# An attention kernel on one core: the causal mask goes from a TensorE matmul into VectorE's row maximum, and a batch element's last row stages run in the first steps of the next

## The chip, the cores and the metric

The kernel runs on one core of one Trainium2 chip. The metric is the device time of one execution in microseconds (us), taken as the median of several runs. The engines are TensorE (PE in the profile; its weight loads are PEld), VectorE (DVE), ScalarE (ACT), GpSimd (POOL) and SyncE (SP), which issues the DMAs. Each has its own queue of instructions, and they wait for each other with semaphores. SBUF is the memory on the core, and the eight PSUM banks (`bank0` to `bank7`) are where TensorE writes.

## The reference

Two layers work on x of 8 batch elements x 512 positions x 128 channels. Each is a modulated layer norm with attention and then one with a feed-forward part, both added to x. Layer 0 (an RWKV scan and a feed-forward in 6-bit numbers) isn't touched. In layer 1, attention has 16 heads and three branches that share the queries:

```python
a1 = _attn(q, k1, v1, causal=True)      # keys from a latent
a2 = _attn(q, ks, vs, causal=False)     # 32 selected keys
a3 = _attn(q, kw, vw, causal=True)      # keys made straight from x
out = g[:, 0] * a1 + g[:, 1] * a2 + g[:, 2] * a3

def _attn(q, k, v, causal):
    s = jnp.einsum('bhqd,bhkd->bhqk', q, k) * scale
    if causal:
        s = jnp.where(mask, s, jnp.finfo(s.dtype).min)
    return jnp.einsum('bhqk,bhkd->bhqd', jax.nn.softmax(s, axis=-1), v)
```

After it comes a recurrent cell over the batch elements, c = f * c + i * g, and an output tanh.

## The kernel before

Layer 1's attention is cut into units. A unit is one head, one of the two causal branches and one tile of 128 query rows; tile t sees (t+1) x 128 keys, so its scores are 128 to 512 columns wide. Four heads make a group; a group has 32 units (`GU`) in two rows of 16 (`RU`), one row per branch; a batch element has four groups, so 128 units, and there are 1024 in all. In a row the tiles come as 3, 2 for each of the four heads, and then 1, 0.

`attend(turn)` exists once for each engine and writes that engine's list by hand, step s after step s. There is no scheduler. It is called for three kinds of turn: `FIRST` (one group), `FULL` (128 units, the body of a hardware loop that runs 7 times) and `LAST` (three groups). The boundary of a turn lies one group ahead of that of a batch element. Step s holds:

- TensorE: the scores of unit s into one of three banks (L1639; a small extra matmul at L1637 for the selected keys); then the mask matmul (L1641), which adds `maskB` to the last 128 columns by multiplying it with an identity, both bf16; the products with the values for rows 11 and 19 steps back (`PV_TALL`, `PV_LOW`, L1601); the spreading of the rows' inverses (`SPREAD`, L1612); the transposes of the probabilities of unit s-2 (`T_LAG`, L1660) into bank 3 or 4; and, from a table in `group_tasks`, one fill task in bank 7 (projections for the next group, the cell and so on: L1507 to L1575; `vl` is L1553).
- VectorE: reads of bank 7 for some tasks; the row maximum of unit s (L1331), which waits for the mask's semaphore `s_qk`; the move of unit s-3's transposed probabilities out of PSUM (`D_LAG`, L1338, tiles 3, 1 and 0); the inverses of a row's sums (`INVERT`), its normalisation (`NORM`, L1314) and the addition (`ADD`, L1320).
- ScalarE: reads of bank 7; the move of tile 2 (L875); where a bank holds selected scores, their copy (L891); the exp of unit s from the bank to `Pb` in SBUF, with the row's sum by an accumulator (L895), which waits for the row maximum; the move of the spread inverses (`MOVE`, L901).

The next transposes wait until the bank that they write has been moved, so TensorE's L1660 at unit k waits for VectorE's L1338 (or ScalarE's L875) of unit k-2. In VectorE's list that move stands behind the row maximum of unit k+1. The scores of unit s wait until the exp of unit s-3 has read their bank.

Stages that lag run past a turn's last unit. Before the change each engine therefore adds steps to each turn, TensorE up to 5, ScalarE 6, VectorE 9, and only then takes the loop's jump (L1691 on TensorE, L1414 on VectorE); L1416 is VectorE's first copy in a turn.

## Time and profile before

| | |
|---|---|
| time, median of 3 runs | 2289.77 us (2286.21 to 2292.29) |
| the profiled execution's own time | 2280.42 us |
| its span | 2278.6 us |
| mean granted clock of TensorE | 0.913 of full speed |
| TensorE, VectorE, ScalarE, GpSimd busy | 85%, 59%, 49%, 28% of the span |
| layer 1's attention | about 380 to 2230 us |

The page's busy times are shares of the span. A matmul's end is modelled, and matmuls overlap, so a line's cost on TensorE is read from the starts in the timeline. "PEld L1660 <- DVE L1338" is idle time of the weight loads at line 1660 that ended when VectorE's L1338 did. "issue" is idle time for which the profile shows no cause outside the engine.

### The profile page before, as it was taken

The numbers are of one execution on the slowest core, as the hardware profiler recorded it, in microseconds if no ns is written. First come the engines' busy times: TensorE is split into PE (matmuls) and PEld (weight loads), VectorE is DVE, ScalarE is ACT, GpSimd is POOL, SyncE is SP. The second block draws the span as 40 slices with busy tenths as digits, with TensorE's granted clock in tenths as the row PEclk, the third lists the DMA queues.
The fourth block names the chain that finished last, engine by engine and source line by source line (L and its number), as shares of the span: only waits on it lengthen the run. The fifth ranks groups of instructions, "written<-read, shape, count | busy, mean of one in ns | idle before, by whom it ended". The sixth has DMA issues, their size and how long they took to land.

```text
span 2278.6 us, 41302 instructions
## 1 busy us (share of the span) xinstructions
PE 1931.2 (85%) x11644; PEld 1110.1 (49%) x11644; DVE 1349.9 (59%) x3206; ACT 1126.1 (49%) x3476; POOL 645.8 (28%) x659
## 2 busy tenths in 40 slices
PE   3333356999989998999899998999899989999995
PEld 2222123555545554555455554555555555555552
DVE  5999942556555555565655564555465645565563
ACT  1112212555546564556555655655465545555551
POOL 0232233333312331333223232323233322332200
PEclk7655665999999999999999999999999999999998
DMA  3000001111101111111111111111111111111101
GB/s 135 0 0 0 0 9 38 51 37 41 48 21 40 39 41 37 34 39 41 44 33 34 46 43 35 34 46 43 35 34 46 43 26 42 36 53 26 41 1 37
DMA packets 71354, 81.39 MB, mean 36 GB/s; under 512 B 29521, under 2 KB 37842, under 8 KB 70994
## 3 DMA queue, kind: packets, MB, share of 16 engines
q1 hardware_dynamic: 71122, 78.55, 13.4%
q8 instruction: 115, 1.88, 0.4%
q14 instruction: 117, 0.96, 0.1%
HBM read 7.70 MB, written 2.10 MB: 4 GB/s over the span
## 4 chain that ended last, share of the span: by engine, by line
PE 74%; DVE 15%; issue 7%; ACT 2%; POOL 1%; SPq 1%; DVEq 1%; DMA 0%; ACTq 0%; POOLq 0%
PE bank L1639 23%; PE bank L1660 14%; PE bank L1601 9%; PE bank L1511 4%; PE bank L1512 4%; DVE arena L1338 3%; PE bank L1641 2%; PE bank L1612 2%; PE bank L1553 2%; PE bank L1507 1%; PE bank L1549 1%; PE bank L1566 1%; DVE arena L1098 1%; DVE arena L1331 1%; PE bank L1574 1%
## 5 line engine op out<-in xcount | busy, mean ns | idle before, releaser
L1331 DVE TENSOR_REDUCE arena<-bank 128x1 f32<-128x512 f32 (+3 forms) x1024 | 501.8, 490 | 681.4 <-PE bank L1641 669.8
L1639 PE MATMUL bank<-arena 96*128 96x512 f32 (+6 forms) x2048 | 782.5, 464 | 44.3 <-issue 33.1
L895 ACT ACTIVATE arena<-bank,arena 128x512 f32<-128x512 f32 (+3 forms) x1024 | 539.7, 527 | 418.3 <-DVE arena L1331 410.9
L1660 PE MATMUL bank<-W,arena 128*128 128x128 f32 x2560 | 480.4, 286 | 38.2 <-DVE arena L1338 33.2
L1660 PEld LDWEIGHTS bank<-W,arena 128*128 128x128 f32 x2560 | 281.3, 142 | 320.9 <-issue 171.3
L1639 PEld LDWEIGHTS bank<-arena 96*128 96x128 f32 x2048 | 336.4, 196 | 189.4 <-issue 146.5
L1338 DVE COPY arena<-bank 128x512 f32<-128x512 f32 (+2 forms) x768 | 351.0, 459 | 0.0
L674 POOL TENSOR_TENSOR arena<-arena,one 128x512 f32<-128x512 f32 x64 | 66.8, 1043 | 846.3 <-DVE arena L1305 836.6
L1641 PE MATMUL bank<-maskB,identB 128*128 128x128 bf16 x1024 | 229.0, 224 | 0.0
L1601 PE MATMUL bank<-arena 128*32 128x256 f32 (+1 forms) x3072 | 222.7, 362 | 3.3 <-DVE arena L1338 2.0
L895 ACT ACTIVATION_READ_ACCUMULATOR arena<-bank,arena 128x1 f32 x1024 | 204.5, 200 | 0.0
L875 ACT ACTIVATE arena<-bank 128x384 f32<-128x384 f32 x256 | 126.0, 492 | 122.4 <-PE bank L1660 122.3
L625 POOL TENSOR_TENSOR arena<-arena,W 128x512 f32<-128x512 f32 x64 | 69.9, 1092 | 342.3 <-ACT arena L817 342.3
L1641 PEld LDWEIGHTS bank<-maskB,identB 128*128 128x128 bf16 x1024 | 100.8, 98 | 115.4 <-issue 87.4
L891 ACT ACTIVATE arena<-bank 128x32 f32<-128x32 f32 (+1 forms) x384 | 78.5, 204 | 142.0 <-DVE arena L1331 140.5
L1462 PE MATMUL bank<-W,arena 128*128 128x128 f32 x160 | 34.0, 349 | 123.3 <-ACT arena L775 53.5
L1601 PEld LDWEIGHTS bank<-arena 128*32 128x32 f32 x3072 | 61.0, 109 | 115.3 <-issue 96.8
L1511 PE MATMUL bank<-arena,LW 96*128 96x512 f32 x192 | 109.3, 652 | 3.1 <-ACT arena L817 2.5
L1512 PE MATMUL bank<-arena,W 128*128 128x512 f32 x192 | 103.8, 623 | 4.3 <-ACT arena L817 3.6
L634 POOL TENSOR_TENSOR arena<-arena 128x512 f32<-128x512 f32 x64 | 81.3, 1271 | 44.0 <-DMA arena<-arena 36.5
L817 ACT ACTIVATE arena<-bank 128x512 f32<-128x512 f32 x128 | 76.6, 599 | 27.1 <-PE bank L1512 9.9
L1462 PEld LDWEIGHTS bank<-W,arena 128*128 128x128 f32 x160 | 23.3, 178 | 135.9 <-ACT arena L775 55.1
(263 smaller groups left out, 2304.2 us busy)
## 6 DMA issues: line engine op xcount, KB each, us to landing
arena<-arena SPq DMA_DIRECT2D x896, 64.0 KB, 2.0
arena<-arena SPq DMA_DIRECT2D x64, 128.0 KB, 2.4
W<-wide SPq DMA_DIRECT2D x1, 3538.0 KB, 12.9
X<-x SPq DMA_DIRECT2D x8, 256.0 KB, 5.4
out<-arena SPq DMA_DIRECT2D x8, 256.0 KB, 2.2
arena<-arena SPq DMA_DIRECT2D x96, 16.0 KB, 1.9
LW<-lat SPq DMA_DIRECT2D x1, 768.5 KB, 13.9
arena<-mods SPq DMA_DIRECT2D x1, 768.0 KB, 4.4
```

Of the source, the lines that this page charges most:

```text
L634: step(pool.tensor_tensor(stX1, rt[:, 2], rt[:, 3], ALU.subtract))
L875: A(turned(turn, k), turned_bank(turn, k), ACT.Copy).then_inc(s_pa, 1)
L891: made = A(p2h[:, h, tiles], scores, ACT.Copy)
L895: A(Pb[:, s % 4, 0:n], bank[s % 3][:, lo:lo + n], ACT.Exp, bias=nmax[:, s:s + 1], accum_out=lsum[:, c:c + 1]).then_inc(s_p, 1)
L1331: v.tensor_reduce(nmax[:, s:s + 1], bank[s % 3][:, lo:lo + n], AX_X, ALU.max, negate=True).then_inc(s_max, 1)
L1338: CP(turned(turn, k), turned_bank(turn, k)).then_inc(s_pd, 1)
L1511: return MM(dst[:], LW[0:QL, col:col + P], latT[0:QL], start=True, stop=True)
L1512: return MM(dst[:], w("wink", col, P), hTc, start=True, stop=True)
L1601: last = MM(bank[5][rows, low * 2 * P:low * 2 * P + n], V[a][turn.g(q) % 2][:, c, rows], PT[low][:, h, c * 2 * P:c * 2 * P + n], start=(c ...
L1639: MM(bank[s % 3][:, 0:lo + n], query(t), Kb[a][0:QD, g % 2, h, skip:skip + lo + n], start=True, stop=False)
L1641: MM(bank[s % 3][:, lo + t * P:lo + n], identB[:], maskB[:], start=False, stop=True).then_inc(s_qk, 1)
L1660: last = pe.transpose(bank[3 + k % 2][:, c * P:(c + 1) * P], Pb[:, k % 4, c * P:(c + 1) * P], ident)
```

## The change

The mask matmul goes, with its two bf16 tiles and the two copies that made them in set-up. In their place the mask lies in SBUF as 512 columns (zero but for the last 128), loaded with the wide input. VectorE's row maximum becomes one `tensor_tensor_reduce`: it adds mask and scores, multiplies by -1, writes the result to `Pb` and takes the minimum, which is the negated row maximum. It is built as two instructions, the fused one and the read of its accumulator, which carries the semaphore. Ahead of it stands an increment of a semaphore of its own (`s_seen`), which takes the waits: for the scores, and for the transposes of unit s-4, since `Pb` is now written here. ScalarE's exp reads and writes `Pb` in place, with scale -1. The scores of unit s now wait for the row maximum of unit s-3, and only where ScalarE copies selected scores from the bank for the exp.

The second part: a turn has no added steps, but for the last one. Stages that lag run in the first steps of the next turn, with negative row and unit numbers. The banks of the scores are renumbered for it, and one fill task (`vl` of group 0) is put three steps earlier.

```diff
@@ -33,7 +33,7 @@
         ("wfT", P), ("ufT", P), ("wiT", P), ("uiT", P), ("wcT", P), ("ucT", P), ("wo2T", P), ("uoT", P),
-        ("cos", T), ("sin", T), ("mask", P), ("iota", KEEP)]
+        ("cos", T), ("sin", T), ("mask", T), ("iota", KEEP)]
 WIDE_AT, _at = {}, 0
@@ -74,7 +74,7 @@
     if g == 0:
-        steps, proj = {"op": 11, "p2T": 23, "o2": 25}, (1, 2, 4, 7, 8, 13, 15, 27, 33)
+        steps, proj = {"op": 11, "p2T": 23, "o2": 25}, (1, 2, 4, 7, 8, 13, 15, 27, 30)
         extra = [] if first else [(17, "z4T"), (20, "gf"), (21, "gi"), (24, "gc")]
@@ -126,6 +126,9 @@
         self.first, self.last = tasks is FIRST, tasks is LAST
+        self.n0 = 0 if self.first else -GU
+        self.n1 = len(self.units) + (ADD - RU + 1 if self.last else 0)
+        self.c0 = (NG - 1) * GU if self.first else 0
 
@@ -148,7 +151,16 @@
         q, h, a, t = self.units[s]
-        return s - s % RU + (NT - 1 - t) * HG + h
+        return self.c0 + s - s % RU + (NT - 1 - t) * HG + h
+
+    def score_bank(self, s):
+
+        return (s if self.first else s + GU) % 3
+
+    def rows(self, s, at):
+
+        r, late = divmod(s - at, RU)
+        return r, late, self.n0 // RU <= r < len(self.units) // RU
 
@@ -227,8 +239,6 @@
         impd = sb("impd", [P, B, B])
-        identB = sb("identB", [P, P], BF16)
-        maskB = sb("maskB", [P, P], BF16)
         ones_row = sb("ones_row", [1, P])
@@ -864,12 +875,12 @@
                 p2h = p2.rearrange("p (t j k) -> p j t k", t=NT, j=HG)
-                for s in range(n_units + MOVE - RU + 1):
+                for s in range(turn.n1):
                     task = turn.at(s - 1, "act")
...
                     k = s - T_LAG
-                    if 0 <= k < n_units and MOVER[turn.units[k][3]] == "act":
+                    if turn.n0 <= k < n_units and MOVER[turn.units[k][3]] == "act":
                         act.wait_ge(s_pT, u0 + (k + 1))
@@ -877,9 +888,6 @@
                         act.wait_ge(s_max, u0 + (s + 1))
-                        if not (turn.first and s < 4):
-
-                            act.wait_ge(s_pT, u0 + (s - 3))
                         if lo:
@@ -887,15 +895,15 @@
                             m = 2 if t == 0 else 1
-                            scores = bank[s % 3][:, 0:m * (KEEP + P)].rearrange("p (m x) -> p m x", m=m)[:, :, 0:KEEP]
+                            scores = bank[turn.score_bank(s)][:, 0:m * (KEEP + P)].rearrange("p (m x) -> p m x", m=m)[:, :, 0:KEEP]
                             made = A(p2h[:, h, tiles], scores, ACT.Copy)
...
                         c = turn.col(s)
-                        A(Pb[:, s % 4, 0:n], bank[s % 3][:, lo:lo + n], ACT.Exp, bias=nmax[:, s:s + 1],
+                        A(Pb[:, s % 4, 0:n], Pb[:, s % 4, 0:n], ACT.Exp, bias=nmax[:, s:s + 1], scale=-1.0,
                           accum_out=lsum[:, c:c + 1]).then_inc(s_p, 1)
-                    r, late = divmod(s - MOVE, RU)
-                    if 0 <= r < n_units // RU and late == 0:
+                    r, late, known = turn.rows(s, MOVE)
+                    if known and late == 0:
                         act.wait_ge(s_sp, turn.r0 + (r + 1))
@@ -1168,8 +1176,6 @@
             step(TS(w("krsw", HALF, HALF), w("krsw", HALF, HALF), 1.0 / HEADS, None, ALU.mult))
-            step(CP(identB[:], w("ident")))
-            step(CP(maskB[:], w("mask")))
             step.settle()
@@ -1300,7 +1306,7 @@
                         v.wait_ge(s_ix, r0 + (r - 1))
-                    step(v.reciprocal(inv[:, r % 2], lsum[:, r * RU:(r + 1) * RU]))
+                    step(v.reciprocal(inv[:, r % 2], lsum[:, turn.c0 + r * RU:turn.c0 + (r + 1) * RU] if r >= 0 else lsum[:, NG * GU - RU:]))
                     step.settle()
@@ -1328,17 +1334,22 @@
                         v.wait_ge(s_qk, u0 + (s + 1))
-                        v.tensor_reduce(nmax[:, s:s + 1], bank[s % 3][:, lo:lo + n], AX_X, ALU.max, negate=True).then_inc(s_max, 1)
+                        if not (turn.first and s < 4):
+
+                            v.wait_ge(s_pT, u0 + (s - 3))
+                        v.sem_inc(s_seen, 1)
+                        v.tensor_tensor_reduce(Pb[:, s % 4, 0:n], bank[turn.score_bank(s)][:, lo:lo + n], w("mask", T - n), -1.0, 3e38,
+                                               ALU.add, ALU.min, nmax[:, s:s + 1]).then_inc(s_max, 1)
                     k = s - D_LAG
-                    if 0 <= k < n_units and MOVER[turn.units[k][3]] == "dve":
+                    if turn.n0 <= k < n_units and MOVER[turn.units[k][3]] == "dve":
                         v.wait_ge(s_pT, u0 + (k + 1))
...
                     for at, row_part in ((INVERT, row_inverted), (NORM, row_normed), (ADD, row_added)):
-                        r, late = divmod(s - at, RU)
-                        if 0 <= r < n_units // RU and late == 0:
+                        r, late, known = turn.rows(s, at)
+                        if known and late == 0:
                             row_part(r)
@@ -1626,28 +1637,29 @@
                                 pe.wait_ge(s_krB, turn.b * (16 * HG) + 16 * HG)
-                        if s >= 3:
-
-                            pe.wait_ge(s_p, u0 + (s - 2))
+                        if s >= 3 or not turn.first:
+
+                            before = s - 2 if s < 2 else s - 3
+                            _, _, a3, t3 = turn.units[before]
+                            pe.wait_ge(s_p if scores_at(a3, t3) else s_max, u0 + (before + 1))
                         lo = scores_at(a, t)
...
 
-                            MM(bank[s % 3][:, lo + n:lo + n + KEEP], query(NT - 1), Kb[0][0:QD, g % 2, h, 0:KEEP],
+                            MM(bank[turn.score_bank(s)][:, lo + n:lo + n + KEEP], query(NT - 1), Kb[0][0:QD, g % 2, h, 0:KEEP],
                                start=True, stop=True)
-                        MM(bank[s % 3][:, 0:lo + n], query(t), Kb[a][0:QD, g % 2, h, skip:skip + lo + n],
-                           start=True, stop=False)
-                        MM(bank[s % 3][:, lo + t * P:lo + n], identB[:], maskB[:], start=False, stop=True).then_inc(s_qk, 1)
+                        MM(bank[turn.score_bank(s)][:, 0:lo + n], query(t), Kb[a][0:QD, g % 2, h, skip:skip + lo + n],
+                           start=True, stop=True).then_inc(s_qk, 1)
                     for low, at, parts in ((0, PV_TALL, 4), (1, PV_LOW, 2)):
-                        r, c = divmod(s - at, RU)
-                        if 0 <= r < n_units // RU and c < parts:
+                        r, c, known = turn.rows(s, at)
+                        if known and c < parts:
                             values(r, low, c)
-                    r, late = divmod(s - SPREAD, RU)
-                    if 0 <= r < n_units // RU and late == 0:
+                    r, late, known = turn.rows(s, SPREAD)
+                    if known and late == 0:
                         spread(r)
                     k = s - T_LAG
-                    if 0 <= k < n_units:
+                    if turn.n0 <= k < n_units:
                         t = turn.units[k][3]
@@ -1720,7 +1732,7 @@
     sin = np.tile(np.sin(angle).T, (HG, 1)).astype(np.float32)
-    mask = np.where(np.arange(P)[None, :] > np.arange(P)[:, None], MASKED, 0.0).astype(np.float32)
+    mask = np.where(np.arange(T)[None, :] - (T - P) > np.arange(P)[:, None], MASKED, 0.0).astype(np.float32)
     cols = [d["L0_c"].T, d["L1_c"].T]
```

VectorE in the loop, four steps from a turn's start. Before:

```order
L1337 ISA [waits probsT_in_psum]
L1338 COPY arena<-bank3 128x4x128 [waits half_pv_done]
L1330 REGISTER_ALU
L1331 TENSOR_REDUCE arena<-bank1 128x1 [waits scores_ready]
L1330 REGISTER_ALU
L1331 TENSOR_REDUCE arena<-bank2 128x1 [waits scores_ready]
L1338 COPY arena<-bank3 128x4x128 [waits half_pv_done,probsT_in_psum]
```

After:

```order
L1336 REGISTER_ALU
L1341 ISA arena<-bank0,W 128x512 [waits scores_ready,probsT_in_psum]
L1341 ISA arena 128x1
L1336 REGISTER_ALU
L1341 ISA arena<-bank1,W 128x384 [waits scores_ready,probsT_in_psum]
L1341 ISA arena 128x1
L1349 COPY arena<-bank3 128x4x128 [waits half_pv_done,probsT_in_psum]
L1336 REGISTER_ALU
L1341 ISA arena<-bank2,W 128x512 [waits scores_ready,probsT_in_psum]
```

Behind every row maximum there is now a second, one-column instruction, and the move of unit s-3 comes behind both. The increment that holds the wait is not a row of its own here.

TensorE at the end of the loop's body (bank 4 and 3: transposes, 7: fill, 5: values, 6: spread). Before, in the steps past the last unit:

```order
L1658 REGISTER_ALU [waits probs_ready]
L1660 MATMUL bank4<-W,arena 128x128 [waits probsT_moved_by_dve]
...
L1553 MATMUL bank7<-LW,arena 128x128 [waits shared_bank_read_by_act]
...
L1601 MATMUL bank5<-arena 32x256 [waits probsT_moved_by_act,probsT_moved_by_dve]
...
L1612 MATMUL bank6<-W,arena 128x128 [waits row_inverses_moved,row_inverses_repeated]
...
L1601 MATMUL bank5<-arena 32x128 x4
L1691 REGISTER_ALU
L1691 COMPARE_AND_BRANCH
```

After, where the jump comes directly behind unit 125's transposes:

```order
L1564 MATMUL bank7<-LW,arena 128x128 [waits shared_bank_read_by_act]
...
L1652 MATMUL bank0<-arena 128x128 [waits row_max_ready]
L1664 REGISTER_ALU
L1670 REGISTER_ALU [waits probs_ready]
L1672 MATMUL bank4<-W,arena 128x128 [waits probsT_moved_by_dve]
L1703 REGISTER_ALU
L1703 COMPARE_AND_BRANCH
```

The last two units' transposes, the two value products and the spread have gone from the end. TensorE at the start of the loop's body, before:

```order
L1639 MATMUL bank0<-arena 128x512 [waits shared_key_moved_odd]
L1641 MATMUL bank0<-maskB,identB 128x128
...
L1511 MATMUL bank7<-arena,LW 128x512 [waits shared_bank_read_by_dve]
L1639 MATMUL bank1<-arena 128x416
L1641 MATMUL bank1<-maskB,identB 128x128
L1639 MATMUL bank2<-arena 128x512
L1641 MATMUL bank2<-maskB,identB 128x128
...
L1660 MATMUL bank3<-W,arena 128x128 [waits probsT_moved_by_dve]
...
L1511 MATMUL bank7<-arena,LW 128x512 [waits shared_bank_read_by_act]
L1639 MATMUL bank0<-arena 128x416 [waits probs_ready]
```

And after:

```order
L1652 MATMUL bank2<-arena 128x512 [waits row_max_ready]
...
L1672 MATMUL bank3<-W,arena 128x128 [waits probsT_moved_by_dve]
...
L1522 MATMUL bank7<-arena,LW 128x512 [waits shared_bank_read_by_dve]
...
L1652 MATMUL bank0<-arena 128x416 [waits row_max_ready]
...
L1672 MATMUL bank4<-W,arena 128x128 [waits probsT_moved_by_dve]
L1652 MATMUL bank1<-arena 128x512 [waits row_max_ready]
...
L1672 MATMUL bank3<-W,arena 128x128 [waits probsT_moved_by_dve]
...
L1652 MATMUL bank2<-arena 128x416 [waits row_max_ready]
...
L1612 MATMUL bank5<-arena 32x256 [waits probsT_moved_by_act]
...
L1623 MATMUL bank6<-W,arena 128x128 [waits row_inverses_moved]
...
L1672 MATMUL bank4<-W,arena 128x128 [waits probsT_moved_by_dve,probs_ready]
...
L1652 MATMUL bank0<-arena 128x512 [waits probs_ready]
```

They stand now between the scores of the new turn's first steps: transposes of units 126 and 127 in steps 0 and 1, values and spread in steps 3 and 4.

## Rows read from the trace of the kernel before

**Rows 1.** The page's sections 1 and 4: busy times, and the chain's shares.
```profile
PE 1931.2 (85%) x11644; PEld 1110.1 (49%) x11644; DVE 1349.9 (59%) x3206; ACT 1126.1 (49%) x3476; POOL 645.8 (28%) x659
...
PE 74%; DVE 15%; issue 7%; ACT 2%; POOL 1%; SPq 1%; DVEq 1%; DMA 0%; ACTq 0%; POOLq 0%
```

**Rows 2.** Windows of 200 us: each engine's busy us (x instructions), granted clock, DMA.
```profile
600.00:800.00 200.00, 188.17 (x1153) 108.44 (x1154) 113.63 (x270) 112.00 (x354) 63.79 (x61) 0.97 0.14 36
```

**Rows 3.** Waits of the whole span: idle us, times, longest; L1639 by shape.
```profile
PEld bank L1660 <- DVE arena L1338: 110.7, 189, 1.1
...
PEld bank L1601 <- DVE arena L1338: 17.5, 34, 1.1
...
L1639 PE MATMUL bank<-arena 96*128 96x512 f32 x512 | 282.4, 634 | 44.3 <-issue 33.1 <-ACT arena L862 9.5 <-ACT arena L895 1.2
```

**Rows 4.** TensorE's timeline near a turn's end: the mask and the next transpose.
```profile
893.29 0.22 PE L1641 MATMUL bank<-maskB,identB 128*128 128x128 bf16 x1
893.35 0.28 PE L1660 MATMUL bank<-W,arena 128*128 128x128 f32 x1
```

**Rows 5.** Timeline around one wait (start us, us, engine, line).
```profile
680.58 0.22 PE L1641 MATMUL bank<-maskB,identB 128*128 128x128 bf16 x1
...
680.84 0.56 DVE L1331 TENSOR_REDUCE arena<-bank 128x1 f32<-128x384 f32 x1 [1.58 <-PE bank L1641]
...
681.31 0.68 DVE L1338 COPY arena<-bank 128x512 f32<-128x512 f32 x1
...
681.83 0.22 PE L1641 MATMUL bank<-maskB,identB 128*128 128x128 bf16 x1
...
682.04 0.42 PEld L1660 LDWEIGHTS bank<-W,arena 128*128 128x128 f32 x4 [0.54 <-DVE arena L1338]
```

**Rows 6.** VectorE's groups by shape: busy us, mean ns of one, idle before.
```profile
L1331 DVE TENSOR_REDUCE arena<-bank 128x1 f32<-128x512 f32 x256 | 176.7, 690 | 208.5 <-PE bank L1641 203.6
...
L1314 DVE TENSOR_TENSOR arena<-bank,arena 128x512 f32<-128x512 f32 x64 | 43.7, 683 | 20.9 <-ACT arena L901 20.9
...
L1252 DVE SCALAR_TENSOR_TENSOR arena<-arena 128x512 f32<-128x512 f32 x8 | 5.5, 682 | 12.2 <-ACT arena L855 12.2
```

**Rows 7.** Timelines: four of VectorE's smallest; ScalarE's accumulator read and its next.
```profile
2233.11 0.37 DVE L948 BATCH_NORM_AGGREGATE small<-small 128x2 f32<-128x6 f32 x4
...
684.76 0.21 ACT L895 ACTIVATION_READ_ACCUMULATOR arena<-bank,arena 128x1 f32 x1
684.86 0.61 ACT L817 ACTIVATE arena<-bank 128x512 f32<-128x512 f32 x1
```

**Rows 8.** Timelines of TensorE and VectorE at L1221, outside the loop and inside.
```profile
2117.72 1.02 PE L1560 MATMUL bank<-W,arena 128*128 128x512 f32 x2
...
2118.78 0.69 DVE L1221 TENSOR_TENSOR arena<-arena,bank 128x512 f32<-128x512 f32 x1 [0.74 <-PE bank L1560]
...
713.52 1.02 PE L1560 MATMUL bank<-W,arena 128*128 128x512 f32 x2
...
714.70 0.69 DVE L1221 TENSOR_TENSOR arena<-arena,bank 128x512 f32<-128x512 f32 x1 [0.79 <-PE bank L1560]
```

**Rows 9.** Timeline where VectorE's move ends just ahead of its reader.
```profile
721.40 0.28 DVE L1338 COPY arena<-bank 128x128 f32<-128x128 f32 x1
...
721.87 0.28 PE L1660 MATMUL bank<-W,arena 128*128 128x128 f32 x1
```

**Rows 10.** TensorE's timeline at a turn's end, with a jump of the loop.
```profile
894.22 0.56 PE L1660 MATMUL bank<-W,arena 128*128 128x128 f32 x3 [0.60 <-DVE arena L1338]
...
903.16 1.22 PE L1639 MATMUL bank<-arena 96*128 96x512 f32 x1 [5.78 <-issue]
```

**Rows 11.** The loop's branch on TensorE's queue: ns min/median/max, first and last start.
```profile
L1691 PEldq COMPARE_BRANCH  x7: 76/3347/3692, 660.8 to 2074.1; - x7
```

**Rows 12.** TensorE's timeline: first scores after the turn's end without a jump.
```profile
2075.16 1.12 PE L1639 MATMUL bank<-arena 96*128 96x512 f32 x2
```

**Rows 13.** Window after the restart: engines' busy us, then TensorE's clock.
```profile
903.10:911.30 8.20, 8.14 (x16) 3.77 (x17) 1.94 (x3) 2.14 (x6) 0.00 (x0) 0.50 0.00 0
```

5 lines of the change are left out of this document (3 added, 2 removed).

## The prediction

> **What bounds the kernel now.** I read the first section of the page, then the chain that ended last, then the table of windows, to find the engine that sets the end; then the waits, to see who holds it up; then the timeline around one of each kind of place. The first section and the chain say TensorE: busy 85% of the span, and 74% of the chain [rows 1]. The windows say where: in the attention of layer 1 TensorE is busy 188 of 200 us, VectorE 114 and ScalarE 112 [rows 2]. Those two are only waited for at single places, so an average tells nothing of them, and the waits do. TensorE's weight loads wait for VectorE's move of the transposed probabilities (L1338) 189 times at the transposes and 34 times at the values: 223 places in 1024 units, 27 or 28 per turn of 128 units [rows 3]. The full-width scores matmul (L1639) sat idle for ScalarE's exp only 1.2 us in all [rows 3], so freeing the scores' bank earlier, which the change also does, is worth about a microsecond and I leave it out.
>
> **Part 1, the mask leaves TensorE.** A mask matmul shows 0.22 us busy, but matmuls overlap: from its start to that of the transpose behind it are 893.29 to 893.35, 0.06 us [rows 4]. Over all such pairs of the trace it is 58 to 60 ns, so 0.059. Its weight load lies beside other matmuls. 1024 x 0.059 would be 60 us. At each of the 223 places where TensorE waits for VectorE's move one mask lies in the wait's shadow, as the one at 681.83 does (TensorE sits idle from then until 682.04 whether it is there or not) [rows 5]. So 1024 - 223 = 801 masks, **-47 us**.
>
> **Part 2, VectorE's row maximum becomes longer.** Take the place at 680.58 [rows 5]. Mask starts 680.58, row maximum of that unit 680.84, the move of an earlier unit stands behind it in VectorE's queue and starts at 681.31, takes 0.68, and the transpose that needed the bank free starts at 682.04, after 0.54 idle. The mask at 680.58 is on this path, ahead of the row maximum, and is among the 801; with it gone the wait is on the scores' matmul. What is new is what stands between the scores' end and the move: the fused instruction in the place of the plain one, its accumulator read as a second instruction, and the wait, which now sits on a semaphore increment of its own ahead of it. I call the sum of the new parts p, per unit.
>
> The main instruction: an addition of a bank and an SBUF tile of 512 columns takes 683 ns, the row maximum of 512 columns 690 [rows 6]. I take them equal. That also holds for the write of the sums to SBUF, which the 683 has and the 690 has not.
>
> The accumulator read, x: no VectorE instruction in the trace reads an accumulator. Below it lie VectorE's smallest: four aggregates in 0.37, one of which takes 0.15, so 0.07 from start to start [rows 7]. Above it lies ScalarE's own accumulator read: 0.19 to 0.21 long, though ScalarE's next instruction starts 0.10 after it [rows 7]. So x is 0.07 to 0.19, and I take 0.07, because start to start is what the queue behind it pays, and both rows say 0.07 to 0.10 there.
>
> The wait, e: the profile has the same instruction with both kinds of wait. At L1221 outside the loop the wait is on the instruction, and it starts 0.04 after TensorE's matmul ends (2117.72 + 1.02 to 2118.78); inside the loop a sequencer operation takes the wait, and it starts 0.15 after (713.52 + 1.02 to 714.70), with VectorE idle for 0.79 before [rows 8]. All 28 in the loop show 0.13 to 0.16 and all 4 outside it 0.04. So e is up to 0.11; I take 0.08, since an increment needs no address worked out. The low end of e is nothing. The increment's second wait, for the transposes of unit s-4, comes two steps after TensorE issued them and is never the last; queued behind the increment are the fused instruction, on which ScalarE's exp waits, and the move, on which TensorE does.
>
> p = 0.15, between 0.07 and 0.30. 223 x 0.15 = **+33 us**. Six more places per turn wait for VectorE's or ScalarE's reads of the shared bank, which stand behind the same instruction: 48 x 0.14 = **+7 us**. Then there are near misses: at 721.40 the move takes 0.28 and ends at 721.68, and the transpose that needs it starts at 721.87 [rows 9]. The trace has about 5 such places per turn with under 0.19 us left; each lies closer by p plus the mask that TensorE no longer does: 40 x 0.1 = **+4 us**.
>
> I work this out as lengthening of waits that exist, not as load, because VectorE has room: 1024 x 0.15 is 154 us on 1350 busy [rows 1].
>
> **Part 3, the late stages of a turn's last rows run in the next turn.** Before the change TensorE does at a turn's end, after its last normal transpose at 893.35 [rows 4], the last transposes at 894.22 (0.60 idle for VectorE's move), then a fill task, values, spread and values again, and then nothing until 903.16, for 5.78 us put down to "issue" [rows 10]. That gap is the loop's jump: TensorE's queue shows a branch of 3.35 us, by the median of 7 [rows 11], and where the same stages end without a jump the next turn's first scores, at 2075.16, have no idle before them [rows 12]. After the restart the clock is at 0.50 (1.2 GHz) for 8.2 us [rows 13]. The branch is issued when the work before it is queued, so the last of it, about 1 us of spread and value matmuls, runs while the jump goes on. Moved past the jump, it costs its own time that was covered, some of it at half clock, and it gives back the 0.60 of waiting and a part of the drain: I put each of the 7 jumps at +0.2, **+1.4 us**. The two turn boundaries without a jump lose the 0.60 wait and the thin tail: -0.8 each, **-1.6 us**. Together nothing. What follows on the other engines: the row inverses (L1303), NORM (L1314) and ADD (L1320) enter VectorE's list in steps 0, 7 and 8 of the next turn behind the first row maxima, ScalarE's MOVE in step 5, and GpSimd's and SyncE's work is behind them as before; no DMA is added or moved past another on SyncE's queue. If their cover were gone, the 0.68 of a NORM 14 times would be 10 us; the first steps have it, since TensorE runs there at half clock. The mask becomes 384 columns wider in a load during set-up, and two set-up copies go: within 0.3 us.
>
> **Sum.** -47 + 33 + 7 + 4 + 0 = -3 us against the profiled execution of 2280.4 us (span 2278.6). That execution lies 9.4 us under the median of the runs, 2289.8, so the same difference on the median gives **2286**. It breaks even at p of 0.16 to 0.17, hence nearly everything hangs on p.
>
> **Rivals.**
>
> *The extra VectorE time is covered.* With p at its lower end, 0.07: 223 x 0.07 = 16, the six places +3, no new near misses: -28 us, 2262. For it: if x is 0.07 and the increment takes the wait at no cost. Against it: the 0.15 at L1221 in the loop.
>
> *Slower: the accumulator read holds VectorE.* If the read takes its whole length (0.19) as ScalarE's shows, and the wait 0.09, p is 0.28: 62 + 13 + 7 - 47 = +36 us, 2326. It is at the same 223 places, where the move stands behind the read in VectorE's queue; it decides from p of 0.20, where the sum is slower by more than 0.3%.
>
> *Half rate.* If the fused instruction took twice as long per column, it would add 0.13 to 0.53 us, 0.33 on average: 223 x 0.33 = 74 us more, and with new waits 2345 to 2400. For it stands only that it reads two tensors and accumulates. Against it: the 683 ns of a bank and an SBUF tile, and of L1252, which reads two float tensors of SBUF in 682 [rows 6]; neither accumulates. The Trainium skill ("Vector Engine (DVE) Microarchitecture Reference", section 7, "Points that are easy to get wrong") says that the scalar-tensor-tensor form with two SBUF sources that are not bf16 halves throughput, because no port is left for the accumulator. L1252's 682 ns speaks against that for the form without accumulator, and here one source is a bank; no run here shows the case with one. By the page's rule, were it to apply, the time would be this rival's 2345 or more; without it the sum is as above.
>
> *The gap at the jump goes.* If it came from the thin tail and not the jump, 5.8 us of idle and some 4 us of half clock would go 7 times: -69 us, 2220. Against it is the branch of 3.35 us itself [rows 11].
>
> **Chances.** Forecast 0.58 (p from 0.11 to 0.21: -13 to +15 us, 2277 to 2305), covered 0.15, slower by the read 0.17, half rate 0.05, gap gone 0.05. The range, 2258 to 2328, holds the forecast, the slower rival's own sum and most of the covered one; the last two rivals lie outside. A measurement of this kernel can tell 0.3% from nothing, 7 us. Faster by more: covered 0.15, gap 0.05, and of the forecast the part with p under 0.13, 0.20: 0.40. Slower by more: 0.17, 0.05, and the part with p over 0.195, 0.10: 0.32. Within: 0.28.
>
> **What would show it.** The move's start behind the row maximum's, 0.47 before for 384 columns, should be 0.47 plus x. The places where TensorE waits for the move: 223 to about 260, the wait about p longer. The chain without L1641, with a larger share of VectorE. All seven gaps at the jumps still there, 5 us or more. A gap under 1 us, a fused instruction of over 0.75 us at 512 columns, or a read that holds the queue 0.15 or more would make the prediction wrong.

## The result, and the profile after

The changed kernel is slower: 2318.07 us by the median of four runs (2311.4 to 2327.2), against 2288.9 for the kernel before. The ratio is 1.0129, with a 95% interval of 1.0084 to 1.0175. The forecast was 2286, no change, with a chance of 0.32 for slower. The time lies in the range, but it moved the other way than forecast, by more than the measurement's uncertainty. Each ratio here and below is taken over executions within 1.5% of their kernel's fastest; only in e13_one_wait does that leave any out, three of ten and the profiled one among them. The profiled execution took 2312.3 us with a span of 2310.5, so the two spans differ by 31.9 us, and the comparison of the traces below is about these.

The page of after, sections 1 and 4:

```profile
PE 1911.7 (83%) x10620; PEld 1069.9 (46%) x10620; DVE 1367.5 (59%) x4228; ACT 1163.8 (50%) x3476; POOL 645.1 (28%) x659
...
PE 69%; DVE 17%; issue 8%; ACT 3%; DVEq 1%; POOL 1%; SPq 1%; DMA 0%; ACTq 0%; POOLq 0%
```

TensorE is busy for 20 us less than in [rows 1], and its share of the chain has gone from 74% to 69% while VectorE's has risen from 15% to 17%. The same in a window of the attention (compare [rows 2], 188 us busy of 200):

```profile
600.00:800.00 200.00, 182.77 (x1043) 101.91 (x1043) 114.67 (x374) 115.85 (x354) 63.73 (x61) 0.96 0.14 36
```

The waits for VectorE's move, which is now at L1349, against the 189 and 34 of [rows 3]:

```profile
PEld bank L1672 <- DVE arena L1349: 226.0, 286, 2.7
...
PEld bank L1612 <- DVE arena L1349: 31.1, 34, 1.4
```

They are 320 places, not 223, and of the larger group the mean wait is 0.79 us where it was 0.59. VectorE's groups by shape, against [rows 6]:

```profile
L1341 DVE CUSTOM_DVE_ANT_0 arena<-bank,W 128x512 f32<-128x512 f32 x256 | 176.7, 690 | 209.6 <-PE bank L1652 151.1 <-PE bank L1672 56.9
...
L1341 DVE DVE_READ_ACCUMULATOR2_ANT arena<- 128x1 f32 x1024 | 85.1, 83 | 0.0
```

The fused instruction of 512 columns takes 690 ns, just as long as the plain row maximum did: half rate is out. Its accumulator read lasts 83 ns. One wait in the timeline, to be read beside [rows 5]:

```profile
920.37 0.52 PE L1652 MATMUL bank<-arena 96*128 96x160 f32 x2
...
921.11 0.29 DVE L1341 CUSTOM_DVE_ANT_0 arena<-bank,W 128x128 f32<-128x128 f32 x1 [1.06 <-PE bank L1652]
...
921.33 0.08 DVE L1341 DVE_READ_ACCUMULATOR2_ANT arena<- 128x1 f32 x1
921.33 0.69 DVE L1349 COPY arena<-bank 128x512 f32<-128x512 f32 x1
...
922.07 0.44 PE L1672 MATMUL bank<-W,arena 128*128 128x128 f32 x2 [0.36 <-DVE arena L1349]
```

The scores end at 920.89 (920.37 + 0.52), and the fused instruction starts at 921.11, 0.22 later. In [rows 5] the mask ended at 680.80 and the row maximum started at 680.84. The accumulator read and the move both start at 921.33: the read stands beside the move and hardly ahead of it. TensorE gets going at 922.07.

Over all units where VectorE had been idle for more than 0.3 us, the median from the scores' end to the start of the row maximum is 37 ns before and 225 ns after. From its start to the move's start it is 208 and 216 ns at 128 columns, 607 and 617 at 512. So the new time per unit is **0.19 of waiting and 0.01 of accumulator read**.

Where in a turn it went can be read from the starts of the 1024 row maxima in both traces. Turns start with one copy on VectorE (columns: count, ns min/median/max, first and last start); before and after:

```profile
L1416 DVE COPY gtc<-gates x7: 169/169/169, 437.7 to 1845.1; 128x3 f32 x7
```

```profile
L1427 DVE COPY gtc<-gates x7: 158/169/171, 430.1 to 1865.2; 128x3 f32 x7
```

That is 234.6 us per turn before and 239.2 after. Of the 4.6 us more, the last eight units and the first eight of the next turn give back 4.2; the units around the fourth part of the third group (units 56 to 63) take 5.2; all the others take 3.5 together. TensorE's granted clock explains the middle figure. The timeline of VectorE, GpSimd and TensorE there, before and then after:

```profile
1003.85 1.51 DVE L1214 TENSOR_SCALAR arena<-W,rankT 128x32 f32<-128x32 f32 x4
...
1004.19 1.12 POOL L643 TENSOR_TENSOR arena<-arena,W 64x512 f32<-64x512 f32 x1 [4.70 <-ACT arena L812]
...
1005.28 1.08 POOL L644 TENSOR_TENSOR arena<-arena,W 64x512 f32<-64x512 f32 x1
...
1005.43 0.69 DVE L1221 TENSOR_TENSOR arena<-arena,bank 128x512 f32<-128x512 f32 x1
...
1006.24 0.29 DVE L1331 TENSOR_REDUCE arena<-bank 128x1 f32<-128x128 f32 x1
1006.45 0.68 DVE L1338 COPY arena<-bank 128x512 f32<-128x512 f32 x1
...
1007.19 0.44 PE L1660 MATMUL bank<-W,arena 128*128 128x128 f32 x2 [0.79 <-DVE arena L1338]
```

```profile
1003.06 2.42 DVE L1220 TENSOR_SCALAR arena<-W,rankT 128x32 f32<-128x32 f32 x4
...
1003.28 1.12 POOL L654 TENSOR_TENSOR arena<-arena,W 64x512 f32<-64x512 f32 x1 [4.79 <-ACT arena L823]
...
1004.36 1.08 POOL L655 TENSOR_TENSOR arena<-arena,W 64x512 f32<-64x512 f32 x1
...
1005.40 0.68 DVE L1227 TENSOR_TENSOR arena<-arena,bank 128x512 f32<-128x512 f32 x1
...
1006.38 0.29 DVE L1341 CUSTOM_DVE_ANT_0 arena<-bank,W 128x128 f32<-128x128 f32 x1 [0.30 <-DVE arena L1227]
...
1006.89 0.69 DVE L1349 COPY arena<-bank 128x512 f32<-128x512 f32 x1 [0.21 <-issue]
...
1007.63 0.67 PE L1672 MATMUL bank<-W,arena 128*128 128x128 f32 x2 [2.27 <-DVE arena L1349]
```

The four selections of L1214 (L1220 after) take 1.51 us before and 2.42 after. GpSimd's two operations (POOL) begin 0.34 us behind the selections' start before and 0.22 behind it after, so one selection or two fall beside them, and each of these lasts 1.1 us. The shared bank's read and the row maximum follow, the move comes last, and TensorE waits 2.27 us for it. Then the granted clock (the third number from the end of a window's row), first before, then after:

```profile
1007.20:1013.70 6.50, 6.50 (x61) 5.23 (x62) 2.19 (x8) 1.97 (x7) 0.60 (x1) 1.00 0.00 0
1013.70:1017.10 3.40, 3.40 (x24) 1.30 (x23) 2.68 (x11) 0.49 (x3) 0.00 (x0) 0.50 0.05 10
```

```profile
1005.42:1007.62 2.20, 0.00 (x0) 0.00 (x0) 1.69 (x6) 0.53 (x3) 1.28 (x2) 1.00 0.01 4
1007.70:1024.70 17.00, 17.00 (x88) 12.43 (x89) 5.02 (x23) 3.61 (x12) 0.00 (x0) 0.50 0.03 5
```

Before, the clock is at 0.50 (1.2 GHz) for 3.4 us here. After, it falls right behind the idle 2.2 us and stays down for 17 us, in which TensorE runs 88 matmuls, 32 of them of 32 columns. Added up over the attention, the stretches at 0.50 are 85 us before and 147 after. The seven turns of after show what a long stretch costs: units 8 to 120 take 201 us in the one turn that has none in its third group, 205 in the one with 6.8 us of it, and 207 to 209 in the five with 13.7 or 17.1. That fits half of the stretch's length, as it must be if TensorE's work takes twice as long there. So the 62 us more are worth some 31 us (an estimate): about as much as the whole difference of the spans, the other terms cancelling each other.

At the jumps the opposite happened:

```profile
897.36 0.28 PE L1672 MATMUL bank<-W,arena 128*128 128x128 f32 x1
900.38 1.22 PE L1652 MATMUL bank<-arena 96*128 96x512 f32 x1 [2.74 <-issue]
```

The gap of 5.78 us in [rows 10] is 2.74 here; the six gaps sum to 33.1 us before and 18.2 after.

### The profile page after: what moved, and what is told of

Read it like the earlier page. It is cut to its first block, busy times and chain, and to the rows that moved or that the text cites. A ratio compares the mean times of both kernels' runs of the same rounds, so it can differ in the third digit from the quotient of the medians.

```text
span 2310.5 us, 40290 instructions
## 1 busy us (share of the span) xinstructions
PE 1911.7 (83%) x10620; PEld 1069.9 (46%) x10620; DVE 1367.5 (59%) x4228; ACT 1163.8 (50%) x3476; POOL 645.1 (28%) x659
## 4 chain that ended last, share of the span: by engine, by line
PE 69%; DVE 17%; issue 8%; ACT 3%; DVEq 1%; POOL 1%; SPq 1%; DMA 0%; ACTq 0%; POOLq 0%
PE bank L1652 21%; PE bank L1672 14%; PE bank L1612 9%; DVE arena L1349 4%; PE bank L1522 4%; PE bank L1523 4%; DVE arena L1341 3%; PE bank L1623 2%; PE bank L1564 2%; PE bank L1545 2%; PE bank L1518 1%; PE bank L1577 1%; PE bank L1560 1%; DVE arena L1106 1%; PE bank L1585 1%
## 5 line engine op out<-in xcount | busy, mean ns | idle before, releaser
L1341 DVE CUSTOM_DVE_ANT_0 arena<-bank,W 128x512 f32<-128x512 f32 (+3 forms) x1024 | 502.0, 490 | 711.4 <-PE bank L1652 573.4
L903 ACT ACTIVATE arena<-arena 128x512 f32<-128x512 f32 (+3 forms) x1024 | 572.8, 559 | 442.5 <-DVE arena L1341 439.2
L1672 PE MATMUL bank<-W,arena 128*128 128x128 f32 x2560 | 487.1, 288 | 97.1 <-DVE arena L1349 92.0
L1672 PEld LDWEIGHTS bank<-W,arena 128*128 128x128 f32 x2560 | 306.2, 142 | 464.3 <-DVE arena L1349 226.0
L1652 PEld LDWEIGHTS bank<-arena 96*128 96x128 f32 x2048 | 341.1, 199 | 174.6 <-issue 149.7
L1349 DVE COPY arena<-bank 128x512 f32<-128x512 f32 (+2 forms) x768 | 356.2, 464 | 2.0 <-issue 1.5
L1612 PE MATMUL bank<-arena 128*32 128x256 f32 (+1 forms) x3072 | 227.6, 369 | 8.3 <-DVE arena L1349 7.7
L903 ACT ACTIVATION_READ_ACCUMULATOR arena<-arena 128x1 f32 x1024 | 194.8, 190 | 0.0
L1473 PE MATMUL bank<-W,arena 128*128 128x128 f32 x160 | 37.5, 379 | 122.2 <-ACT arena L786 52.7
L645 POOL TENSOR_TENSOR arena<-arena 128x512 f32<-128x512 f32 x64 | 81.4, 1271 | 39.0 <-DMA arena<-arena 31.9
L1473 PEld LDWEIGHTS bank<-W,arena 128*128 128x128 f32 x160 | 26.3, 195 | 135.3 <-ACT arena L786 54.3
L1341 DVE DVE_READ_ACCUMULATOR2_ANT arena<- 128x1 f32 x1024 | 85.1, 83 | 0.0
L649 POOL TENSOR_TENSOR arena<-arena 128x512 f32<-128x512 f32 x64 | 81.3, 1270 | 5.0
## 6 DMA issues: line engine op xcount, KB each, us to landing
W<-wide SPq DMA_DIRECT2D x1, 3730.0 KB, 13.3
```

Of the source, the lines that this page charges most:

```text
L645: step(pool.tensor_tensor(stX1, rt[:, 2], rt[:, 3], ALU.subtract))
L649: pool.tensor_tensor(stX2, rt[:, 0], rt[:, 1], ALU.add).then_inc(s_rope, 1)
L903: A(Pb[:, s % 4, 0:n], Pb[:, s % 4, 0:n], ACT.Exp, bias=nmax[:, s:s + 1], scale=-1.0, accum_out=lsum[:, c:c + 1]).then_inc(s_p, 1)
L1341: v.tensor_tensor_reduce(Pb[:, s % 4, 0:n], bank[turn.score_bank(s)][:, lo:lo + n], w("mask", T - n), -1.0, 3e38, ALU.add, ALU.min, nmax[: ...
L1349: CP(turned(turn, k), turned_bank(turn, k)).then_inc(s_pd, 1)
L1612: last = MM(bank[5][rows, low * 2 * P:low * 2 * P + n], V[a][turn.g(q) % 2][:, c, rows], PT[low][:, h, c * 2 * P:c * 2 * P + n], start=(c ...
```

## The experiments

**The two parts apart.** `e1_stages` has the moved stages alone, `e2_mask` the mask on VectorE alone.

```diff
 e1_stages, against after (its other lines put back the mask's two tiles and the exp from the bank)
...
-v.sem_inc(s_seen, 1)
-v.tensor_tensor_reduce(Pb[:, s % 4, 0:n], bank[...][:, lo:lo + n], w("mask", T - n), ...)
+v.tensor_reduce(nmax[:, s:s + 1], bank[turn.score_bank(s)][:, lo:lo + n], AX_X, ALU.max, negate=True)
...
+MM(bank[turn.score_bank(s)][:, lo + t * P:lo + n], identB[:], maskB[:], start=False, stop=True)
```

> Only the second part of the change: the late row stages run in the next turn's first steps, the mask stays a TensorE matmul. The prediction put this part at nothing (within 3 us of before). The trace of after says otherwise: around a jump a turn is 4.2 us shorter, 2.65 of them idle (the gap of 5.8 became 2.7) and the rest half clock. If that is the stages' doing, this kernel is 25 to 32 us faster than before, near 2260. If the long half-clock stretch at the third group of a turn (17 us from 1007.7 in after, 3.4 us in before) comes from the stages, it is here too and the time is near 2285.

`e2_mask` is the kernel before with the VectorE, ScalarE and set-up hunks of the change and TensorE's new wait ahead of the scores, and without its hunks on `n0`, `n1`, `rows` and `score_bank`:

```diff
 e2_mask, against before
-v.tensor_reduce(nmax[:, s:s + 1], bank[s % 3][:, lo:lo + n], AX_X, ALU.max, negate=True)
+v.sem_inc(s_seen, 1)
+v.tensor_tensor_reduce(Pb[:, s % 4, 0:n], bank[s % 3][:, lo:lo + n], w("mask", T - n), ...)
...
-MM(bank[s % 3][:, lo + t * P:lo + n], identB[:], maskB[:], start=False, stop=True)
```

> Only the first part: mask added by VectorE with the row maximum, turns with their extra steps as before. Theory of the wait (VectorE starts 0.22 us behind the scores' end instead of 0.04, at about 320 places): 22 to 27 us slower without any change of the clock, near 2313. Theory of the clock (the same part also makes TensorE sit idle 2.3 us in the third group, and the half-clock stretch behind it grows from 3.4 to 17 us): 28 us more, near 2340. If the clock's fall came from the moved stages, this kernel keeps before's 3.4 us and stays near 2313.

Measured: e1_stages 2267.2 us, ratio to before 0.9888 (0.9853 to 0.9923); e2_mask 2324.8, ratio 1.0145 (1.0104 to 1.0185). So the first part loses 1.4% and the second gains 1.1%, where the prediction had -3 us and nothing. In e1_stages all units between 8 and 112 of a turn take the same time as before, to 0.01 us in eight units, but for the third group's clock (4.9 us at 0.50 for 3.4, by the mean of seven turns); the gain is at the turns' ends alone. In e2_mask the long stretch of half clock is there (13.7 us in most turns, 160 us in all), and with half the length of its half-clock stretches taken off each, the units 8 to 120 of a turn take 2.1 us more than before. The clock's fall therefore comes from the mask's part.

**The price of the mask and of the increment.**

```diff
 e4_nomask, against before
-           start=True, stop=False)
-MM(bank[s % 3][:, lo + t * P:lo + n], identB[:], maskB[:], start=False, stop=True).then_inc(s_qk, 1)
+           start=True, stop=True).then_inc(s_qk, 1)
 e5_inc, against before
+v.sem_inc(s_seen, 1)
 v.tensor_reduce(nmax[:, s:s + 1], bank[s % 3][:, lo:lo + n], AX_X, ALU.max, negate=True).then_inc(s_max, 1)
```

> Before without the mask matmul, and so without the causal mask in the result: the price of the masks on TensorE alone. The prediction's term is 801 masks at 0.059 us, 47 us, so 2243. If masks also shorten the path scores to row maximum to move at the waits, up to 60 us, 2230. If TensorE's waits for VectorE swallow them, under 25 us.

> Before with one instruction more in VectorE's list: a semaphore increment of its own ahead of each row maximum, which takes the wait for the scores. All else as before, the mask on TensorE. The prediction's e was 0.08 us per unit: 223 places, 18 us and a few for new waits, near 2312. The trace of after shows the fused instruction 0.22 us behind the scores' end, 0.18 more than before: 40 us and 10 to 20 for new waits, near 2345, and more if the clock falls longer. If the 0.18 belongs to the fused instruction and not to the increment, under 10 us.

Measured: e4_nomask 2230.0 us, ratio 0.9723 (0.9687 to 0.9760), 63 us by the ratio and 58 by the medians; e5_inc 2356.3, ratio 1.0285 (1.0244 to 1.0327), 65 us slower. So 1024 semaphore increments on VectorE's queue cost as much as the 1024 mask matmuls on TensorE. Its place in the timeline of e5_inc:

```profile
1026.99 0.22 PE L1643 MATMUL bank<-maskB,identB 128*128 128x128 bf16 x1
...
1027.36 0.42 DVE L1333 TENSOR_REDUCE arena<-bank 128x1 f32<-128x256 f32 x1 [0.48 <-PE bank L1643]
```

The mask ends at 1027.21 and the row maximum starts at 1027.36; the median over the idle places is 0.155 us, 0.12 more than before. With the half clock taken off as above, the units 8 to 120 of a turn take 3.7 us more, 30 us in eight turns (222 places wait for the move, and 222 x 0.12 is 27); the half clock, 174 us against 85, makes up the rest. Both masks and increment thus have a price on the path near what their steps in the timeline show, and then a second one through the clock that only the increment has (88 us at half clock in e4_nomask).

**The second wait on the increment.** In after it also waits for unit s-4's transposes; `e13_one_wait` leaves that wait out.

```diff
 e13_one_wait, against after
-if not (turn.first and s < 4):
-    v.wait_ge(s_pT, u0 + (s - 3))
 v.sem_inc(s_seen, 1)
```

> After with the increment waiting for the scores alone; its second wait, for the transposes of unit s-4, is left out, since TensorE has ended those before the scores that it waits for. In after the fused instruction starts 0.225 us behind the scores' end (median), with one wait on the increment and a plain row maximum 0.155. If the second wait makes the difference, 0.155 here, and with about 320 waits for VectorE some 20 us less than after, near 2295. If the fused instruction makes it, 0.225 and the time of after, 2318.

Measured: 2288.8 us by the median of ten runs that lie far apart (2263.6 to 2302.1), ratio to before 0.9983 (0.9954 to 1.0013). The median from scores to fused instruction is 0.196 us. So of the 0.19 us that after adds there, 0.12 belongs to the increment, 0.03 to its second wait and 0.04 to the fused instruction. (At 112 of after's 656 idle places the profile names the transposes of L1672 as the last to be waited for; by the median the fused instruction starts 0.225 us behind the scores' end there too.) These 0.03 us move the ratio from 1.0129 to 0.9983. Neither expectation fits: the start is between the two, and the gain is more than 0.03 us at 304 waits. The clock can make up the difference from turn to turn. TensorE's idle in the third group is 1.92 us here, and in the trace two turns of seven pass it without the long half clock and take 231 and 232 us, where the other five take 236 to 241. That trace is of an execution of 2300.4 us; how many turns fell in the shorter ones isn't known.

**What lets the clock fall.**

```diff
 e8_pick, against after
-if g == 2 and at == 24:
-    for j in range(NT):
-        last = pick(turn.nb, j)
...
+if g == 2 and 20 <= at < 20 + NT:
+    last = pick(turn.nb, at - 20)
...
```

> After with VectorE's four selections of the third group (L1220) one per step in steps 20 to 23, not all four in step 24, where two of them took 1.1 us each beside GpSimd's work and the shared bank's read and the row maximum stood behind them. Theory of the clock: TensorE's idle 2.3 us there is what lets the clock fall for 13.7 to 17.1 us; without it the stretch is 3.4 us or none, and the kernel is 25 to 30 us faster than after, near 2290. Rival: the fall comes from the work itself (32 matmuls of 32 columns) at whatever idle: the stretch stays and the gain is the 0.9 us per turn of the stalled selections, under 10 us.

Measured: 2288.8 us (2282.4 to 2307.2), ratio to before 1.0024 (0.9996 to 1.0051), 29 us faster than after. The place in its timeline, and the clock behind it:

```profile
1002.92 0.69 DVE L1227 TENSOR_TENSOR arena<-arena,bank 128x512 f32<-128x512 f32 x1 [1.37 <-PE bank L1571]
...
1003.91 0.29 DVE L1341 CUSTOM_DVE_ANT_0 arena<-bank,W 128x128 f32<-128x128 f32 x1 [0.30 <-PE bank L1652]
...
1004.41 0.69 DVE L1349 COPY arena<-bank 128x512 f32<-128x512 f32 x1 [0.21 <-issue]
...
1005.16 0.44 PE L1672 MATMUL bank<-W,arena 128*128 128x128 f32 x2 [1.40 <-DVE arena L1349]
```

```profile
1005.20:1020.00 14.80, 13.90 (x102) 8.80 (x103) 8.69 (x37) 6.42 (x20) 1.07 (x2) 1.00 0.06 10
```

TensorE still idles 1.40 us, but in this turn the clock stays at 1.00 through the same 32-column matmuls. Over the traces, one execution of each kernel, stretches of 13.7 or 17.1 us at 0.50 follow this point in none of the seven turns with 0.79 us of idle (before, e1_stages, e9_pad), 0.91 (e4_nomask) or 1.40 (e8_pick), in three with 1.49 (e6_move_first, below), in five with 1.75 (e5_inc), five with 1.92 (e13_one_wait), six with 1.97 (e2_mask) and five with 2.27 (after). So the long fall came only behind the longer idle here, and not behind every one; with the shorter idle the same work shows 3.4 us, none, or 6.8 (three turns of e1_stages). Two of e8_pick's ten executions took 2307 us at a mean clock of 0.904, against 2282.9 and 0.911 for the traced one; what the clock did in them isn't known. The Trainium skill ("SBUF — State Buffer", "Who interferes with whom") says that a tensor_scalar in a 2-port mode and a GpSimd instruction lock each other out for a whole instruction. After's trace agrees as far as it goes: the selection that starts at 1003.36 ends at 1004.44, just behind GpSimd's operation (1003.28 to 1004.40), and takes 1.08 us instead of 0.23. That the selections run in such a mode isn't shown.

**The gap at the jump.** In before one more load of instructions falls between the jump and the first scores (q8 is a queue that loads instructions; columns: packets, MB, share; the window is 900.2 to 903.1):

```profile
q8 instruction: 1, 0.02, 2.7%
```

`e9_pad` adds 24 increments that nobody waits for, ahead of the loop on TensorE, and nothing else.

```diff
+for _ in range(24):
+    pe.sem_inc(s_pad, 1)
 with pe.Fori(0, B - 1) as i:
     attend(Turn(FULL, i))
```

> Before with 24 semaphore increments, that nobody waits for, in TensorE's list just ahead of the loop: nothing else. In before a load of instructions (16 KB, 900.48 to 901.73 in the trace) stands between the loop's jump and the first scores, and TensorE starts at 903.16, 3.06 us after the last wait of its sequencer; in the kernels whose TensorE list has another length it starts 0.1 us after. Theory of the code's position: the loop's top lies near the end of a loaded piece of code, and 24 more instructions ahead of it shift it into the next, so the gap goes from 5.2-5.9 to about 2.8 and the kernel is 15 to 30 us faster, near 2265. Theory of the stages (the gap shrinks because the late stages are gone from the end): the gap stays above 5 and the time within 5 us of before.

Measured: 2272.7 us, ratio 0.9926 (0.9900 to 0.9951): 24 instructions more make the kernel 17 us faster. Its timeline at the same jump:

```profile
897.42 0.43 PE L1602 MATMUL bank<-arena 128*32 128x128 f32 x8
900.58 0.69 PE L1640 MATMUL bank<-arena 96*128 96x512 f32 x1 [2.73 <-issue]
```

All gaps of e9_pad are 2.7 to 3.2 us, with every stage where it was, and the half clock behind the jump lasts 6.8 us instead of 10.2. The loads' times agree with the theory. At each of before's six jumps the branch ends 3.0 to 3.5 us ahead of the first scores, and a load on q8 runs between, ending 1.2 to 1.4 us ahead of them. In e9_pad the branch ends 0.6 us ahead, and that load starts only behind the first scores' start. The increments aren't free: at the loop's entry, where before has no such gap, e9_pad has one of 3.1 us and 6.8 us of half clock. The kernels with before's TensorE list (e5_inc, 5.5 to 6.0, and e11_move_first_only below, 5.2 to 6.2) keep the long gap; those whose list has another length (e4_nomask and e2_mask, 2.9 to 4.4) have a shorter one without moved stages. The six gaps sum to 17.2 us in e9_pad and 17.0 in e1_stages. So most of what the second part gained is the position of the loop's top in the loaded code. The Trainium skill ("Advanced Engine Details and Errata", "ISA Cache") gives 16 KB, 256 instructions, as the size of a line of the instruction cache. The load in the trace agrees: it is one packet of 16 KB, 0.02 MB when rounded. Between e1_stages and e9_pad 0.4% is left for the stages themselves, at intervals that overlap.

**The order on VectorE.** If the increment and the row maximum only hurt because the move stands behind them, the move can go first.

```diff
 e6_move_first, against after: the block of the move stands ahead of the row maximum, and goes from behind it
+k = s - D_LAG
+if turn.n0 <= k < n_units and MOVER[turn.units[k][3]] == "dve":
+    ...
+    CP(turned(turn, k), turned_bank(turn, k)).then_inc(s_pd, 1)
 if s < n_units:
     ...
     v.sem_inc(s_seen, 1)
```

`e7_stages_move_first` has the same swap against e1_stages, `e11_move_first_only` against before; there the block stands ahead of the plain row maximum.

> After with VectorE's move of unit s-3 ahead of the fused row maximum of unit s, not behind it. Theory of the wait: the increment and the row maximum cost TensorE time only because the move stands behind them, so the 320 waits go, and with them the 2.3 us idle in the third group and the long half-clock stretch: 60 us or more faster than after, near 2240. Rival: the waits only change sides, since the row maximum now stands behind the move and the exp comes late for its transposes: within 15 us of after.

> The stages moved, the mask on TensorE, and VectorE's move ahead of the row maximum: the same swap of two instructions where there is no increment. Theory of the wait: 209 places with 0.6 us of wait on the weight loads go in part, 20 to 50 us faster than the stages alone (2267). Rival as in the run before: within 10 us of 2267.

> Before with VectorE's move ahead of the row maximum and nothing else. The same swap was worth 88 us on the stages-moved kernel with the mask on TensorE (2267 to 2179) and 135 us on after. If it is worth the same here, 2200. If the moved stages are needed for it, clearly above 2215.

| kernel | move behind the row maximum | move first |
|---|---|---|
| before | 2289 | 2222.6, ratio 0.9699 (0.9676 to 0.9722) |
| e1_stages | 2267 | 2178.7 (e7), ratio 0.9522 (0.9506 to 0.9537) |
| after | 2318 | 2183.0 (e6), ratio 0.9539 (0.9493 to 0.9585) |

The waits for the move, in e6_move_first and then e7_stages_move_first:

```profile
PEld bank L1672 <- DVE arena L1339: 60.6, 102, 1.9
...
PEld bank L1612 <- DVE arena L1339: 23.2, 35, 1.2
```

```profile
PEld bank L1675 <- DVE arena L1346: 56.9, 128, 0.8
...
PEld bank L1614 <- DVE arena L1346: 6.1, 8, 0.9
```

In e6_move_first these are 137 places and 84 us of weight loads' idle, where after had 320 and 257; in e7_stages_move_first 136 and 63, where e1_stages had 209 and 118. On after and on e1_stages the gain, 135 and 88 us, is more than the expectations had: the increment's 0.19 us no longer stands ahead of the move, and most of the old waits of 0.6 us go with it.

On before it is less: 67 us, not the 88 of e1_stages, and 2222.6 lies above the 2215 from which the expectation called the moved stages needed. The traces put the difference at the jumps. The units 8 to 120 of a turn take 190 us in both e11_move_first_only and e7_stages_move_first, but the six gaps sum to 34.3 us in the first and 12.8 in the second. With the move first, then, the second part of the change is worth 44 us, not 21. How much of that is again the code's position wasn't tested.

**All together.** `e10_move_first_pick` is e6_move_first with the edit of e8_pick; `e12_stages_move_pick` is e7_stages_move_first with that edit, so the mask is on TensorE.

> After with VectorE's move ahead of the row maximum and the four selections one per step. The move alone gave 2183, with half-clock stretches of 13.7 us left in the third group of some turns. If these hang on VectorE's crowded step as in after, they go: 20 us faster, near 2163, and faster than the same order with the mask on TensorE (2179). If they hang on the work itself, 2175 to 2185.

> The stages moved, VectorE's move first, the selections one per step, and the mask still a TensorE matmul: the same as the fastest kernel so far (2167) but for where the mask is added. If the mask matmul costs its 60 us (58 measured by leaving it out of before) wherever VectorE isn't waited for, this is 2167 plus 30 to 60, near 2210. The kernel with the mask on TensorE and the old selections took 2179, with half-clock stretches of 3.4 us only, so the selections can give little: theory of the remaining waits, 2170 to 2180, so that the mask's move is worth 5 to 15 us even then.

Measured: e10_move_first_pick 2166.8 us, ratio 0.9453 (0.9423 to 0.9483); e12_stages_move_pick 2177.8, ratio 0.9525 (0.9507 to 0.9544). The first is the fastest kernel of this study, 5.5% faster than before. As the first of its expectations had it, none of its third groups has a stretch of 13.7 us (three of seven in e6_move_first). The page of e10 and a stretch of its timeline:

```profile
PE 1834.3 (85%) x10620; PEld 1059.8 (49%) x10620; DVE 1370.0 (63%) x4228; ACT 1146.6 (53%) x3476; POOL 645.2 (30%) x659
...
PE 71%; DVE 12%; issue 9%; ACT 5%; POOL 1%; DVEq 0%; SPq 0%; DMA 0%; ACTq 0%; POOLq 0%
```

```profile
916.29 0.64 PE L1612 MATMUL bank<-arena 128*32 128x256 f32 x8
916.59 0.42 DVE L1348 CUSTOM_DVE_ANT_0 arena<-bank,W 128x256 f32<-128x256 f32 x1 [0.33 <-PE bank L1652]
...
916.86 0.44 PE L1672 MATMUL bank<-W,arena 128*128 128x128 f32 x2
...
917.33 0.42 DVE L1339 COPY arena<-bank 128x256 f32<-128x256 f32 x1 [0.32 <-PE bank L1672]
```

The move at 917.33 now follows the transposes at once, and the fused instruction runs beside TensorE's work. Adding the mask on VectorE is worth 0.7% here by the ratios (0.5%, 11 us, by the medians). With the old order it cost 1.4% on before and 2.4% with the stages moved (1.0129 against 0.9888), and with the move first but the old selections it gives nothing (2183.0 against 2178.7). It doesn't reach the 50 to 60 us that leaving out the masks gave on before. The units 8 to 120 of a turn take 187.8 us in e10 and 190.0 in e12, but the gaps at the jumps (21.4 us against 13.3) and the half clock over the attention (65 us at 0.50 against 44) take back a part.

## Why the prediction was wrong

- **The masks, -47 us.** Right within its size. e4_nomask gave 58 to 63 us, of which 11 are the gaps at the jumps (33 us before, 22 there), so about 50. The price of 0.059 us was read from masks with a transpose behind them; the trace has 366 with a value product behind them, where start to start is 0.15, and the prediction didn't look at those.
- **x, 0.07 us for the accumulator read.** It was 0.01 from start to start. The bound from VectorE's smallest instructions was too high, and the upper end, from ScalarE's read, was far off. The page "VectorE: DVE Perf Modes" of the Trainium skill has the read as an instruction of its own ("Two Vector instructions with no wait between them"): it is, with 83 ns, and costs the queue nearly nothing.
- **e, 0.08 us for the wait.** It was 0.19. The row at L1221 showed 0.11 [rows 8], and I went below it with a reason of my own; the increment alone has 0.12. That two waits on one increment and the fused instruction add 0.07 was shown nowhere in the trace of before.
- **p, 0.15.** It was 0.20, just at the point that the slower rival named as deciding. That rival had the right place (the move behind the row maximum, at the 223 waits) and nearly the right time, 2326, but the wrong carrier: the read holds nothing, the wait does.
- **The near misses, 40 places.** There were 97 more waits. The prediction counted places with under 0.19 us left, and let each come closer by p and one mask. The runs separate the two: with the increment alone there are 222 places (e5_inc), without the masks 254 (e4_nomask), with the whole first part 331 (e2_mask). So the new waits come above all where TensorE is faster. That the masks of several units add up ahead of a wait would explain it, but no run shows that.
- **The clock.** It was in the sum only behind the jumps. This is the step that failed by most: a change of the clock elsewhere stood in the sum as nothing, and 62 us more at 0.50 made it about 31 us. The window in [rows 13] showed what half clock does, and the 3.4 us at 1013.7 in each turn of before showed that the third group sits near the fall; the prediction looked at neither as something that the change could move. That longer waits are paid twice, once as idle and once as clock, was missing.
- **Part 3, nothing.** The boundaries gave 1.1%. The step that failed here was to take all 5.78 us as the jump because the branch took 3.35 [rows 10, 11]: the branch ends at 899.6 and TensorE starts at 903.16, and the 3.5 us between had no cause in my account. The rival "the gap goes" was given 0.05 on that ground, and half of it came true, though for the code's position and not for the thin tail. Also, there are six jumps back, not seven: the shortest branch, 76 ns [rows 11], is the loop's exit.
- **The total.** The sum was -47 for the masks, +44 for the waits, 0 for the jumps and 0 for the clock. The traces have some -50, -15 for idle at the jumps and +31 for the clock; the spans' +32 then leaves 66 for the waits (an estimate, the remainder). The masks were right, p was 25% low, and the last two terms were absent. They are opposite in sign and each many times the forecast difference, so that the result lies only 1.4% from the forecast is luck.

## What to carry to other kernels

Ask of every instruction that is made longer what stands behind it in its own queue, and whether that could stand ahead: here the swap of two instructions was worth 3% to 6%, more than the change itself. Count a wait of the bounding engine twice where it is long or near a place at which the clock already falls, and look at the clock for each stretch before and not only for the span. When two kernels differ at a loop's jump, compare the loads of instructions before crediting the edit: code moved by 24 instructions was worth 0.7%.

## What was not expected of the hardware

A wait on a semaphore increment ahead of an instruction started that instruction 0.12 us later than the same wait on the instruction itself (0.155 us behind the scores' end against 0.037), and 0.19 later with two waits and the fused instruction behind it (0.225). The fused addition and minimum from a bank and an SBUF tile ran at the row maximum's rate (690 ns for 512 columns), and its accumulator read cost 8 to 10 ns of the queue. A loop's jump back cost TensorE 5.2 to 5.9 us of idle or 2.7 to 3.2, by the position of the code. In the third group TensorE's clock fell for 14 to 17 us in five or six turns of seven where TensorE had sat idle for 1.75 to 2.27 us, in three at 1.49, and in none at 1.40 or less. Why one turn falls and another with the same idle doesn't isn't settled by these runs.
